# A two-layer conditioned transformer kernel: the normalised attention rows are turned one slot later, in two other banks, behind the projections' first half

## What is computed

```python
def _ada_rmsnorm(x, t, gamma_w, beta_w):
    return (t @ gamma_w.T) * _rmsnorm(x) + (t @ beta_w.T)

# layer 0 (t is the condition), 16 heads of 16
x = x + a_alpha * _attention(_ada_rmsnorm(x, t, ...), W_q, W_k, W_v, W_o)
x = x + f_alpha * _swiglu(_ada_rmsnorm(x, t, ...), gate_w, hidden_w, out_w, out_b)   # hidden 1024
# layer 1
h = x * (scale * rsqrt(mean(x * x) + EPS))
val, gate = split(h @ up_w.T)                       # 2 x 1024
h = val * gelu(gate)
y = act_quant(h) @ weight_quant(down_w).T + x
```

## Time and profile before

| | us |
|---|---|
| median of 3 runs | 1160.73 |
| lowest, highest | 1156.8, 1166.3 |
| the profiled execution | 1168.0 |
| its span (first to last instruction) | 1166.2 |
| granted TensorE clock, mean of the span | 0.963 of full speed |

### The profile page before, as it was taken

The page is one execution under the profiler, slowest core; times in us unless marked ns, Lnnn a source line. Parts: engine busy times, 40 slices in busy tenths (PEclk is TensorE's granted clock), DMA queues, the critical chain, the costliest instruction groups (busy, mean ns, idle before and its releaser), DMA issues.

```text
span 1166.2 us, 19073 instructions
## 1 busy us (share of the span) xinstructions
PE 1057.0 (91%) x6775; PEld 728.6 (62%) x6775; DVE 793.7 (68%) x1617; ACT 556.7 (48%) x1242; POOL 302.8 (26%) x372
## 2 busy tenths in 40 slices
PE   5779689998998999899999989997998999899997
PEld 4424135774675577467556746753776788788775
DVE  2676468668767856876785687667645886567775
ACT  2346356456645645664665556455553322222221
POOL 2302003221321322232132113211222444233331
PEclk9779789999999999999999999999998999999998
DMA  6463452624616261561626145251111111002111
GB/s 216 144 110 75 89 88 88 115 29 104 128 48 107 75 127 20 107 129 54 105 67 135 19 91 119 64 104 58 39 55 50 55 55 42 27 29 73 55 50 37
DMA packets 87965, 92.69 MB, mean 79 GB/s; under 512 B 10448, under 2 KB 85208, under 8 KB 86848
## 3 DMA queue, kind: packets, MB, share of 16 engines
q1 hardware_dynamic: 87056, 90.70, 34.4%
q10 hardware_dynamic: 816, 0.79, 0.2%
HBM read 61.68 MB, written 29.78 MB: 78 GB/s over the span
## 4 chain that ended last, share of the span: by engine, by line
PE 74%; DVE 13%; issue 5%; DMA 3%; POOL 2%; ACT 2%; SPq 1%; POOLq 0%; ACTq 0%; DVEq 0%
PE gen L1054 29%; PE core L1054 13%; PE pvb L1157 10%; PE core L1131 8%; PE core L1145 7%; DVE negmax L818 6%; PE gen L1365 2%; DVE xn L794 1%; PE pvb L1357 1%; PE gen L1112 1%; DMA v_d<-v 1%; ACT xn L617 1%; DMA shift_d<-shift 1%; POOL stat L518 1%; DMA xa<-in_x_dram 1%
## 5 line engine op out<-in xcount | busy, mean ns | idle before, releaser
L818 DVE TENSOR_REDUCE negmax<-core 128x1 f32<-128x512 f32 x512 | 338.2, 685 | 190.6 <-PE core L1131 189.6
L629 ACT ACTIVATE p<-core 128x512 f32<-128x512 f32 x512 | 278.2, 597 | 165.8 <-PE core L1145 163.5
L1131 PE MATMUL core<-kst,qst 96*128 96x512 bf16 x512 | 197.1, 403 | 44.7 <-DVE negmax L818 28.9
L1054 PE MATMUL gen<-hs,wgh 128*128 128x256 f32 x1536 | 219.9, 293 | 8.9 <-DVE a L872 8.9
L1054 PEld LDWEIGHTS gen<-hs,wgh 128*128 128x128 f32 x1536 | 195.6, 189 | 27.6 <-DVE a L872 13.2
L1054 PE MATMUL core<-wup,hp 128*128 128x512 f32 x768 | 193.2, 401 | 0.5 <-POOL hp L581 0.5
L538 POOL TENSOR_TENSOR a<-a 128x256 fp32r<-128x256 f32 x128 | 94.1, 735 | 329.8 <-ACT a L647 329.8
L1145 PE MATMUL core<-qst,kst 99*128 99x512 bf16 x512 | 160.1, 394 | 2.8 <-DMA qst<-shift_d 2.8
L1054 PEld LDWEIGHTS core<-wup,hp 128*128 128x128 f32 x768 | 141.2, 190 | 29.2 <-issue 0.9
L1131 PEld LDWEIGHTS core<-kst,qst 96*128 96x128 bf16 x512 | 46.9, 98 | 166.2 <-DVE negmax L818 79.5
L1157 PE MATMUL pvb<-p,vst 128*32 128x512 f32 x1024 | 129.8, 626 | 0.0
(11 more groups left out here) (151 smaller groups left out, 1181.3 us busy)
## 6 DMA issues: line engine op xcount, KB each, us to landing
parts_d<-qk SPq DMA_DIRECT2D x32, 384.0 KB, 2.6
qst<-parts_d SPq DMA_DIRECT2D x90, 128.0 KB, 4.7
kst<-parts_d SPq DMA_DIRECT2D x90, 128.0 KB, 8.1
v_d<-v SPq DMA_DIRECT2D x8, 1024.0 KB, 11.2
vst<-v_d SPq DMA_DIRECT2D x16, 512.0 KB, 5.7
xa<-in_x_dram SPq DMA_DIRECT2D x8, 512.0 KB, 5.1
xr<-in_x_dram SPq DMA_DIRECT2D x8, 512.0 KB, 3.9
x_d<-x SPq DMA_DIRECT2D x8, 512.0 KB, 6.1
```

Of the source, the lines that this page charges most:

```text
L629: act.activation(p32[:, ring(b, m), k * S:(k + 1) * S], stb[k], ACT.Exp, scale=SCALE).then_inc(s["exp_"], 1)
L818: dve.tensor_reduce(negmax[:, n // TT, n % TT:n % TT + 1], smb[n % 2], AX_X, ALU.max, negate=True).then_inc(s["smax"], 1)
L1054: last = pe.matmul(out_, l, r, start=start and i == 0, stop=stop and i == len(passes) - 1, **kw)
L1131: pe.matmul(smb[n % 2], qst[0:KROWS, h, q * P:(q + 1) * P], kst[0:KROWS, h, :], start=True, stop=True).then_inc(s["smax_mm"], 1)
```

## The change

The second norm's transposition moves from slot 9 to slot 10, in front of the third q/k projection, and everything that hangs on it moves one slot later: affine to 11, high and low part to 12. For all inputs but the last it writes gen[0] and gen[1] in place of gen[2] and gen[0] (`turned_bank`). The fourth q/k projection moves from slot 11 to 12 and to bank gen[0], the third to bank gen[2]; the two halves of v from 12 and 13 to 13 and 14 and to gen[1] and gen[2]. The waits on bank releases follow the banks. The whole diff:

```diff
--- before.py
+++ after.py
@@ -56,7 +56,7 @@
 
     STEPS = 2 * H
     T_SQ1, T_XN1, T_XT1, T_H1, T_HH1, T_HL1 = 1, 2, 3, 4, 5, 5
-    T_QK, T_V = (7, 8, 10, 11), (12, 13)
+    T_QK, T_V = (7, 8, 10, 12), (13, 14)
     T_MAX = 18
     GROUP = 4
     T_TURN = [T_MAX + 2 * GROUP * (g + 1) for g in range(H // GROUP)]
@@ -64,7 +64,7 @@
     T_PV = T_ST + 2
     T_OT = T_PV + STEPS + 2
     T_OP = (T_OT + 3, T_OT + 4)
-    T_SQ2, T_XN2, T_XT2, T_H2, T_HH2, T_HL2 = [T_OT + n for n in (6, 7, 8, 9, 10, 10)]
+    T_SQ2, T_XN2, T_XT2, T_H2, T_HH2, T_HL2 = [T_OT + n for n in (6, 7, 9, 10, 11, 11)]
 
     T_GH = [T_OT + 13 + n - (n > 5) for n in range(NCH)]
     T_DOWN = [t + 2 for t in T_GH]
@@ -210,7 +210,7 @@
         down_bank = gen[1][:, D:2 * D]
         qt_bank = pvb[:, :].bitcast(BF16)
 
-        XT_BANK, QK_BANK, V_BANK, OT_BANK, OP_BANK = (2, 0), (0, 1, 1, 2), (0, 2), (0, 1), (1, 2)
+        XT_BANK, XT2_BANK, QK_BANK, V_BANK, OT_BANK, OP_BANK = (2, 0), (0, 1), (0, 1, 2, 0), (1, 2), (0, 1), (1, 2)
         Y_BANK = 2
         wbank = gen + [pvb]
         up_bank = smb + stb
@@ -219,6 +219,10 @@
         def two_banks(b, pair):
 
             return (0, 2) if b == B - 1 else pair
+
+        def turned_bank(b, i):
+
+            return XT_BANK if i == 1 or b == B - 1 else XT2_BANK
 
         def gh_bank(b, n):
             return gen[0] if b == B - 1 else gen[n % 2]
@@ -799,9 +803,9 @@
                     need(dve, f"xt{i}", KD, b, k + 1)
                     scale = cur[:, c, gamma * KD + k:gamma * KD + k + 1]
                     if beta is None:
-                        dve.tensor_scalar(h32[:, k, :], gen[XT_BANK[k]][:, :], scale, None, ALU.mult).then_inc(s[f"h32_{i}"], 1)
+                        dve.tensor_scalar(h32[:, k, :], gen[turned_bank(b, i)[k]][:, :], scale, None, ALU.mult).then_inc(s[f"h32_{i}"], 1)
                     else:
-                        dve.tensor_scalar(h32[:, k, :], gen[XT_BANK[k]][:, :], scale, cur[:, c, beta * KD + k:beta * KD + k + 1],
+                        dve.tensor_scalar(h32[:, k, :], gen[turned_bank(b, i)[k]][:, :], scale, cur[:, c, beta * KD + k:beta * KD + k + 1],
                                           ALU.mult, ALU.add).then_inc(s[f"h32_{i}"], 1)
 
             def tiles(t):
@@ -1087,7 +1091,7 @@
                 last.then_inc(s["cw2_t"], 1)
                 pe.wait_ge(s["cw2_tc"], 2)
 
-                pe.wait_ge(s["qk_r"], 2 * KD)
+                pe.wait_ge(s["v_h"], 1)
                 for i in range(NSC - NFIRST):
                     for k in range(KD):
                         n = i * KD + k
@@ -1109,7 +1113,7 @@
                 need(pe, f"xn{i}", TT, b, TT)
                 for k in range(KD):
                     for t in range(TT):
-                        last = pe.transpose(gen[XT_BANK[k]][:, t * P:(t + 1) * P], xn[:, t, k * P:(k + 1) * P], ident[:, :])
+                        last = pe.transpose(gen[turned_bank(b, i)[k]][:, t * P:(t + 1) * P], xn[:, t, k * P:(k + 1) * P], ident[:, :])
                     last.then_inc(s[f"xt{i}"], 1)
 
             def col(pair, k, a, n):
@@ -1171,7 +1175,7 @@
                     if b == 0:
                         pe.wait_ge(s["qkv_lo"], len(WG_QKV))
 
-                for name, per, other, k in ((), (("xt_", 2, b - 2, 1),), (("qk_r", 2 * KD, b, 2),), (("h32_2", KD, b - 2, 1), ("xt_", 2, b - 2, 2)))[j]:
+                for name, per, other, k in ((), (("xt_", 2, b - 2, 1),), (("xt_", 2, b - 2, 2),), (("h32_2", KD, b - 2, 1), ("qk_r", 2 * KD, b, 1)))[j]:
                     need(pe, name, per, other, k)
                 col0 = ((j % 2) * KD + j // 2) * P
                 exact(gen[QK_BANK[j]][:, :], [(col(wqkv, k, col0, P), col(hp, k, 0, S)) for k in range(KD)]).then_inc(s["qk_mm"], 1)
@@ -1179,7 +1183,7 @@
             def project_v(b, j):
                 if j == 0:
                     need(pe, "h32_2", KD, b - 2, 2)
-                need(pe, "qk_r", 2 * KD, b, (1, 2 * KD)[j])
+                need(pe, "qk_r", 2 * KD, b, (2, 3)[j])
                 for t in range(2):
                     last = exact(gen[V_BANK[j]][:, t * D:(t + 1) * D],
                                  [(col(hp, k, (2 * j + t) * P, P), col(wqkv, k, 2 * D, D)) for k in range(KD)])
@@ -1211,6 +1215,8 @@
                 c, j = n // KF, n % KF
                 if n == 0:
                     need(pe, "hl2", KD, b, KD)
+                    need(pe, "qk_r", 2 * KD, b + 2, 2 * KD)
+                if n == 1:
                     need(pe, "v_h", TT // 2, b + 2, 1)
                 need(pe, "a_", NCH, b, n if b == B - 1 else n - 1)
                 for k2 in range(2):
@@ -1301,12 +1307,12 @@
                     for c in range(2):
                         for b in at(z, T_OP[c]):
                             project_o(b, c)
+                    for b in at(z, T_XT2):
+                        need(pe, "qk_r", 2 * KD, b + 2, 2)
+                        norm_t(b, 2)
                     for j, t in enumerate(T_QK):
                         for b in at(z, t):
                             project_qk(b, j)
-                    for b in at(z, T_XT2):
-                        need(pe, "qk_r", 2 * KD, b + 2, 1)
-                        norm_t(b, 2)
                     for j, t in enumerate(T_V):
                         for b in at(z, t):
                             project_v(b, j)
```

## The result

| | before | after |
|---|---|---|
| median of 4 runs | 1161.08 | 1195.76 |
| lowest, highest | 1156.8, 1166.3 | 1188.61, 1199.04 |
| ratio, 95% interval | | 1.0264 [1.0218, 1.0309] |
| profiled execution, its span | 1168.0, 1166.2 | 1194.75, 1192.9 |
| granted clock, mean of the span | 0.963 | 0.956 |

The change makes the kernel slower by 2.6%. 1160.73 times the ratio is 1191.4, where 1183 was forecast. Three figures for the size stand beside each other: the ratio says 30.6, the two medians of the table 34.7 (1195.76 taken by itself is 12.8 above the forecast and 1.8 above the top of its range), and the two profiled spans 26.7, where 22.4 was forecast. Four runs of each kernel spread over 9.5 and 10.4.

The account below looks back on a forecast made before the run. A ring bounds it: gate in slot 18, TensorE's work, fourth projection, split, loads, gate. Six periods 21.6, iteration 0 +1.4, iteration 7 +0.5, start -1.1 sum to 22.4; 1160.7 + 22.4 = 1183, range 1169 to 1194.

Parts of the forecast that it names:

- A: Slots 10 to 18: fourth part set's split comes 3.6 later per period and delays the gate equally; 1183, chance 0.66.
- rival C: TensorE's clock falls in each of six periods, 6 x 1.6 = 9.6 on top of A, 1193; chance 0.12.
- anchor: Shift turning of slot 10: stays at 395.95, released by VectorE's two maxima; removing the 0.84 wait gains none.
- step 1: Slot 10: transposes stand before the third projection, 1.0 until the next instruction; it starts at 399.7 in place of 398.70.
- step 2: VectorE, slot 11: two maxima to 403.0, affine to 404.4, third remainder to 405.1, before at 402.71.
- Step 3: Slot 12: fourth projection at 403.7 in place of 401.00, 2.7 later: transposes 1.0, scores 0.9, rest waiting for VectorE.
- Step 4: ScalarE: its own full queue puts the fourth set's middle part at 410.2 in place of 406.53, 3.6 later.
- Step 6: SyncE's queue to slot 18: the 15.6 from split to gate stay; gate at 427.6 in place of 424.0, wait about 2.2.
- Step 7: Iteration 0: fourth projection behind slot 11's maxima, +1.4; iteration 7: transposes leave a VectorE shadow, +0.5.
- Step 8: Start: second V projection needs only the third set's remainder, 1.1 earlier, tables and weight turning follow: -1.1.
- Rival B: Slots 12 to 14: VectorE and ScalarE catch up, only TensorE's part is paid; +12, 1173, chance 0.10.
- Rivals D and E: D: the 15.6 to the gate shrink, no difference, 1162, 0.08. E: slot 9's 0.84 wait is gained, 1155, 0.04.

Follow-up runs that it names:

- experiment 4: Kernel before with only the fourth q/k projection moved to slot 12 and the halves of v to 13 and 14: 1184.63, ratio 1.0191.
- experiment 3: Changed kernel with the projections back in their old slots, transposition still in slot 10: 1211.23, ratio 1.0405 to the kernel before.
- experiment 1: Kernel before with the twelve loads of tile 0 put ahead of the stores of part sets 2 and 3: 1157.01, ratio 0.994.
- experiment 2: Changed kernel with the twelve loads put ahead of the stores of part sets 2 and 3: 1167.0, ratio 1.0033 to the kernel before.
- experiment 5: Changed kernel with sixteen unused identity transposes filling TensorE's wait before the shift's turning: 1191.35, ratio 1.0212 to the kernel before.

## Why the prediction was right, and in which terms it was off

The direction and the chain were the ones named: a fourth split that comes later, and a gate that the loads behind it open 15 to 16 later. By its number the result is no clean hit of A. 1191.4 lies above A's own range, 1177 to 1189, and next to rival C, 1193; it lies in the stated range because this one took in most of C. In the profiled spans two errors of A covered for the clock in part: a split forecast too late (3.2 in six periods), and a start 3.9 shorter, which is scatter. That part is luck. Point by point, from the turning of slot 10 on:

- **The anchor, step 1 and step 2 held.** The turning waits 2.05 in all six places (2.0 forecast), the transposes cost 1.0 (third projection at 3.73, forecast 3.75), the affine comes at 6.90 (forecast 7.05). Removing the 0.84 brought nothing by itself.
- **Step 3 held.** The fourth projection is 2.7 later, as forecast. Its parts (1.0 transposes, 0.9 scores, 0.8 wait for VectorE) are no prices of their own: in experiment 4 the slot of scores alone, with no transposes, costs 1.96, with a wait of 0.94 for VectorE in it, and in experiment 3 the transposes without the slot put the fourth projection back by the same 2.7.
- **Step 4 is the term that was mis-sized**, and with it 5. Forecast +3.6, measured +3.06 for the split where the clock is kept, 15.49 behind the turning (16.0 forecast); with a fall it ends at 17.1. The reading "before, ScalarE waited for slot 13's scores; now its own queue is full" was wrong: the queue was full before as well. The row of the exponentials in the earlier trace rows ends at 405.57 + 1.09 = 406.66, behind the start of the middle part at 406.53. And the six instructions in front of the middle part were added by their busy times, 5.10 from those of the view above, while they start 4.56 apart; the same overlap, 0.13, stands in the two rows just named. These 0.54 make up the difference between 3.6 and 3.06.
- **Step 6 held.** Split to gate is 15.2 to 15.8, the gate's wait 1.82 to 2.34 (2.0 to 2.5 forecast). Experiments 1 and 2 show that the order of the queue makes this wait: with the loads ahead of the stores both kernels pass slot 18 without one. TensorE's own lateness, put at 2.7, is the 2.16 of experiment 2; the other 1.0 of the 3.1 per period is the longer wait for the loads.
- **Step 7**: +0.9 in iteration 0 for +1.4. **Step 8**: the first maxima came at 41.55 in place of 43.59, 2.0 earlier for 1.1. The first turning is 3.9 earlier, but experiment 1, whose program is that of before up to there, has it at 94.35 too. So this term can't be told from the scatter of single executions.
- **The clock was the term left out of the sum.** Rival C put falls in each of the six slots 10, 6 x 1.6 = 9.6. They came in three of six, 5.0 in all; another 4.9 came where nothing was forecast, between gate and next turning. Together 9.9: the size of C, half of it in another place. One of the two rows that C's price rested on was misread. The fall in 677 to 680 does not stand behind an idle time of 2.0; TensorE had waited 0.79 and 0.78 there:

```profile
676.20 0.39 PE L1131 MATMUL core<-kst,qst 96*128 96x512 bf16 x1 [0.79 <-DVE negmax L818]
...
678.02 0.45 PE L1131 MATMUL core<-kst,qst 96*128 96x512 bf16 x1 [0.78 <-DVE negmax L818]
```

  So the kernel before already had falls without a long wait, and the price of 1.6 is that of such a fall. It was right all the same: 1.65 in slot 10. The Trainium skill, "TensorE: Matmul & The Clock Gate", Part 1, says that the array's default clock is the low one, that activity lifts it, and that a long wait between matmuls makes the following ones run cold. Here the trace agrees behind the wait of 2.05 in three of six places, and experiment 5 shows the wait to be the cause of those. The page does not say that every wait of this size does so. That by its rule each period would meet a low clock was the prediction's own step, and the trace contradicts it in the other three.

Forecast against measured, in spans: six periods 21.6 for 18.4; start, iteration 0 and the rest +0.8 for about -1.6; clock 0 for 9.9. The errors partly cancel. Rival B, TensorE's part alone, was put at +12; with the ring cut TensorE's part measures 6 x 2.16 = 13.0 from turning to gate. The spans of that pair differ by 7.3 only, since the falls of the clock lie otherwise in the two. Rivals D and E are out: the interval excludes both.

What stays open: in which iterations the falls in slot 10 come (1, 3, 5 after; 2, 4, 6 in experiment 2; only 4 in experiment 3), and, apart from those right behind the wait in slot 18, which stretches from gate to next turning have one. With that, it is open too how the greater part of the 19.4 came back with the loads moved. A different order on ScalarE, with the high parts of `hs` behind the middle part of the fourth set, wasn't tried.

## What to carry to other kernels

When a queue in fixed order carries both the transfers that the next stage waits for and stores that come late, look at what is queued in front of the load that ends last, before any computation is moved: two moves in the DMA order were worth 1.1% here, and moving the work on TensorE cost 2.6%, or 0.9% when both kernels have the loads first. A wait in front of an engine isn't a gain to be had if the engine it waits for has no hole; what counts is how far the move puts back the step that closes the ring. Size the wait of a full in-order engine by the distances of the starts, not by the sum of the busy times, and after cutting one DMA wait look for the next transfer of the same queue.

## What was not expected of the hardware

- With the same instructions and the same wait of 2.05, the granted clock fell in one iteration and not in the next, in strict alternation in the changed kernel and in experiment 2. In experiment 2, where no wait for loads disturbs the rhythm, the five periods from the gate of iteration 1 on alternate accordingly: 104.9, 103.3, 104.9, 103.3, 104.9. In experiment 3, with the same wait, only one of six had a fall.
- Falls can be moved by filling a wait: experiment 5 removed three of 1.65 and found more of 1.5 later in the same periods.
